# The same instructions on tiles that stand in another order in SBUF (a graph network in split fp32r products, one core)

## The reference

```python
h   = x @ W0 + b0                          # 256x256 weights
x1  = layernorm(x + (adj @ h) / adj.sum(-1, keepdims=True))
y1  = relu(adj @ (x1 @ W1) + b1)
y2  = relu(adj @ (y1 @ W2) + b2)
y3  = adj @ (y2 @ W3) + b3
out = layernorm(x1 + y3)                   # no gain, no bias, eps 1e-5
```

## Time and profile before

| | |
|---|---|
| median of three runs | 562.41 us |
| the profiled execution: its time | 563.61 us |
| its span in the trace | 561.8 us |
| TensorE busy with matmuls | 540.8 us, 3648 matmuls |
| TensorE busy with weight loads | 499.1 us, 3648 loads |
| VectorE, ScalarE, GpSimd busy | 356.8, 273.7, 197.8 us |

### The profile page before, as it was taken

One profiled execution on the slowest core, in us unless ns is written; L12 is line 12 of the kernel. 1 busy time (PEld: TensorE's weight loads), 2 busy tenths in 40 slices (PEclk: granted clock), 3 DMA queues, 4 the chain that ended last, 5 costly groups with the idle time before them and its releaser, 6 DMA issues.

```text
span 561.8 us, 10399 instructions
## 1 busy us (share of the span) xinstructions
PE 540.8 (96%) x3648; PEld 499.1 (89%) x3648; DVE 356.8 (64%) x1082; ACT 273.7 (49%) x645; POOL 197.8 (35%) x216
## 2 busy tenths in 40 slices
PE   3789999999999999999999999999999999999996
PEld 3768998989989898998989999898998989899885
DVE  4586575766747566674757657576674756657555
ACT  4156536454453645446364543645445364543532
POOL 1131807135090622608054180713509063261000
PEclk9899999999999999999999999999999999999999
DMA  6531050320505013050410405022050501300002
GB/s 204 189 90 62 1 187 2 101 88 1 188 0 179 8 55 132 0 187 0 134 52 24 163 0 187 0 90 97 0 187 0 175 13 54 134 1 39 1 1 75
DMA packets 19525, 43.53 MB, mean 77 GB/s; under 512 B 1968, under 2 KB 10928, under 8 KB 19504
## 3 DMA queue, kind: packets, MB, share of 16 engines
q1 hardware_dynamic: 19360, 43.00, 22.8%
q10 hardware_dynamic: 144, 0.26, 0.2%
HBM read 34.87 MB, written 8.39 MB: 77 GB/s over the span
## 4 chain that ended last, share of the span: by engine, by line
PE 92%; DVE 3%; DMA 2%; ACT 1%; issue 1%; SPq 0%; DVEq 0%
PE bank_b L154 16%; PE bank_a L154 15%; PE bank_b L155 15%; PE bank_a L156 15%; PE bank_a L155 15%; PE bank_b L156 15%; DMA adj_raw<-in_adjT 1%; DMA xT_raw<-in_xT 1%; DVE adj_lo L496 1%; DVE v L544 0%; DVE x_lo L496 0%; DVE stats L552 0%; DVE x L548 0%; DVE h_lo L496 0%; SPq L169 0%
## 5 line engine op out<-in xcount | busy, mean ns | idle before, releaser
L686 POOL TENSOR_TENSOR adj_lo<-adj_raw,adj_hi 128x512 fp32r<-128x512 f32 x56 | 70.9, 1299 | 281.6 <-ACT adj_hi L347 281.6
L496 DVE TENSOR_TENSOR x_lo<-bank_a,x_hi 128x512 fp32r<-128x512 f32 x64 | 44.3, 692 | 68.3 <-ACT bank_a L410 68.3
L154 PE MATMUL bank_b<-h_hi,adj_hi 128*128 128x258 f32 x256 | 73.3, 286 | 5.7 <-DVE h_lo L496 3.9
L155 PE MATMUL bank_b<-h_lo,adj_hi 128*128 128x258 f32 x256 | 73.4, 287 | 0.0
L156 PE MATMUL bank_b<-h_hi,adj_lo 128*128 128x258 f32 x256 | 72.7, 284 | 0.0
L154 PE MATMUL bank_b<-s_hi,adj_hi 128*128 128x256 f32 x256 | 71.8, 280 | 0.9 <-DVE s_lo L496 0.9
L155 PE MATMUL bank_b<-s_lo,adj_hi 128*128 128x256 f32 x256 | 71.4, 279 | 0.0
L156 PE MATMUL bank_b<-s_hi,adj_lo 128*128 128x256 f32 x256 | 71.4, 279 | 0.0
L385 ACT ACTIVATE std<-moments,eps_col 128x1 f32<-128x1 f32 x64 | 18.9, 295 | 101.2 <-DVE moments L560 101.2
L428 ACT ACTIVATE std<-moments,eps_col 128x1 f32<-128x1 f32 x64 | 18.9, 295 | 81.8 <-DVE moments L600 81.8
L679 POOL TENSOR_TENSOR x1b<-x,b_all 128x256 f32<-128x256 f32 x64 | 46.0, 752 | 30.6 <-DVE x L548 30.6
(11 more groups left out here) (72 smaller groups left out, 1551.4 us busy)
## 6 DMA issues: line engine op xcount, KB each, us to landing
adj_raw<-in_adjT SPq DMA_DIRECT2D x32, 512.0 KB, 5.5
xT_raw<-in_xT SPq DMA_DIRECT2D x32, 256.0 KB, 5.8
x_raw<-in_x SPq DMA_DIRECT2D x16, 512.0 KB, 6.4
out_y<-y SPq DMA_DIRECT2D x15, 512.0 KB, 2.9
w_raw<-in_w SPq DMA_DIRECT2D x3, 256.0 KB, 6.1
out_y<-y SPq DMA_DIRECT2D x4, 128.0 KB, 1.9
w_raw<-in_w ACTq DMA_DIRECT2D x1, 256.0 KB, 2.7
b_all<-in_b SPq DMA_DIRECT2D x2, 128.0 KB, 7.2
```

Source lines behind the costliest of these rows:

```text
L154: pe.matmul(acc, st[0], mv[0], start=start, stop=False)
L155: pe.matmul(acc, st[0], mv[1], start=False, stop=False)
L496: return dve.tensor_tensor(lo, full, hi.bitcast(F32), ALU.subtract)
L686: pool.tensor_tensor(adj_lo[:, s, k, :], adj_raw[:, k, :], adj_hi[:, s, k, :].bitcast(F32), ALU.subtract).then_inc(adj_split, 1)
```

## The change

The declarations of eight names are put in another place. No instruction, wait, shape, type or loop is changed.

```diff
         w_hi, w_lo = pair("w", [P, 4, KF, F])
+        xT_hi, xT_lo = pair("xT", [P, KF, N])
         adj_hi, adj_lo = pair("adj", [P, RING, T, N])
+        h_hi, h_lo = pair("h", [P, T, F + ONES])
         x1_hi, x1_lo = pair("x1", [P, T, F])
-        s2_hi, s2_lo = pair("s2", [P, T, F])
-
-
-        inv_rows = sb("inv_rows", [P, T], F32)
-        std1 = sb("std1", [P, T], F32)
-
-        xT_hi, xT_lo = pair("xT", [P, KF, N])
         g_hi, g_lo = pair("g", [P, KF, N])
         x2_hi, x2_lo = pair("x2", [P, KF, N])
+        s2_hi, s2_lo = pair("s2", [P, T, F])
         x3_hi, x3_lo = pair("x3", [P, KF, N])
         s3_hi, s3_lo = pair("s3", [P, T, F])
-        h_hi, h_lo = pair("h", [P, T, F + ONES])
...
         y = sb("y", [P, T, F], F32)
+        inv_rows = sb("inv_rows", [P, T], F32)
         stats1 = sb("stats1", [P, T, 6], F32)
...
         moments2 = sb("moments2", [P, T, 2], F32)
+        std1 = sb("std1", [P, T], F32)
         std2 = sb("std2", [P, T], F32)
```

## The result

The changed kernel takes 566.73 us, the median of four runs (566.22 to 567.36), against 562.4 us for the kernel before (562.33 to 563.61): a ratio of 1.0073, with a 95% interval of 1.0055 to 1.009. It is slower by 3 to 5 us, and the forecast was 566.9.

What follows compares the result with a forecast made beforehand. TensorE, never waiting mid-run, was taken as the bound, time being the sum of matmul pitches. Only p2 and p5 added, +4.5 us, to the median 562.41, giving 566.9 us; range 557.5 to 571.0, the forecast's own 564.5 to 568.5.

Steps and rivals of the forecast that it cites:

- p2 and p5: 512-column products, stationary x1 or s2, moving adj: 5.60 us each, +0.28 us a step, +4.5 us in all.
- "I take the pair", the rests modulo 128: All products: pitch judged by whether both operands' starts are odd or even multiples of 64 bytes; no size of its own.
- p3, p4, p6, p7 at 0: Products whose operands keep their rests: no change; bounds -0.40 us a step for p6, p3, p7, +0.11 for p4.
- p0 at 0: 256-column product whose operands come to the same rest: no change; at most 0.01 us a step gained, 0.10 lost.
- p1 at 0: 258-column product reading h and adj: no change; bounds -4.1 us and +0.6 us over 16 graphs.
- VectorE and the others at 0: VectorE, ScalarE and GpSimd on moved tiles: no change; 7% more VectorE work uncovered at the ends is about 1 us.
- Placement is inert: All products: level comes from product order alone, step stays 33.39 us, time 562.4 us; chance 0.25.
- Faster through `h`: p1 falls to 114.3 ns, -0.25 us a step, 558.3 us; includes p6, p3 or p7 dropping; chance 0.20.
- Slower still: p2 and p5 at 233.3 ns, p0 and p4 at 117.9 too: +3.4 us on top, 570.3 us; chance 0.10.
- rival 3: Same as Slower still: p0 and p4 at 117.9 ns add +3.4 us, 570.3 us; chance 0.10.
- rival 2: Same as Faster through `h`: p1 faster, 558.3 us; its side part is p6, p3 or p7 dropping; chance 0.20.
- theory A: From the experiments' expectations, all products: operand starts set the pace, and the product ahead passes its level on; no single size.

Runs made afterwards that it cites:

- x1_s2_64_clean: Kernel before with x1 and s2 moved by 64 bytes, every other large tile kept modulo 256: 565.31 us against 563.21, ratio 1.0032.
- same_rests: Tile order of the kernel after, unused spacers restoring the starts modulo 128 of the kernel before: 563.01 us against 563.05, ratio 0.9996.
- same_rests_256: Tile order of the kernel after, eight unused spacers restoring the starts modulo 256 of the kernel before: 563.11 us against 563.21, ratio 0.9997.
- the sweeps: Two separate programs, TensorE alone, groups of 12 matmuls: one varies the stationary start, the other also the moving start; 512 columns at multiples of 256 bytes: 226.6 to 226.7 ns.
- x1_s2_even: Kernel after with x1 and s2 put back on multiples of 128 by spacers: 565.92 us against 563.05 for the kernel before, ratio 1.005.
- sweep_rest: Separate program, TensorE alone, stationary start 0 to 1024 bytes past the moving one, steps of 32, up and back; 256 columns at 64 bytes: 118.1 or 113.8 ns.
- g0_s3_192: Kernel before with spacers putting g at 0 and s3 at 192 modulo 256: 565.68 us, ratio 1.0043.

## Why the prediction was right, and where it was wrong

- **The time: 566.9 forecast, 566.73 measured.** The closeness of the two is luck. The step grew by 0.20 us and not by 0.28, and what made up the 0.20 was not the sum that the forecast wrote down. The step explains 3.2 of the 4.3 us between the medians; the other 1.1 isn't in it, and is of the size of the spread between executions (562.33 to 563.61 for the kernel before).
- **p2 and p5: right, in place and size.** 5.60 us each was forecast, and 5.60 each is what they take, 233.3 ns a matmul. That a distance of 64 bytes costs this is borne out by the sweep (233.4 ns at 64, 227.8 to 226.7 at 0) and by x1_s2_64_clean. This term alone is the forecast's +4.5 us. The row that it took the price from fits only by luck: modulo 256, p3 stands at 192 and not at 64. At 192 the sweep has 229.2 to 230.2 ns, and p3 itself takes 229.0 in the kernel after and 233.6 in the kernel before, with the same two operands at the same distance. At 229.2 to 230.2 ns the same sum would have given +1.3 to +2.1 us, by estimate.
- **"I take the pair", the rests modulo 128: wrong.** The period is 256 bytes: same_rests missed p2 by 0.15 us, same_rests_256 missed nothing. The places of p2 and p5 are the same by either rule, since `x1` and `s2` went from distance 0 to 64; the likeness to p3 holds by the rule of 128 alone.
- **p3, p4, p6, p7 at 0: wrong, by -0.36 us a step for p3, p6 and p7 and +0.11 for p4.** The prediction saw the passing on in the rows near the end and gave bounds for it, -0.40 and +0.11, which both came about almost in full. It should have carried them into the likeliest case: it forecast a new pace for p2 and, behind it, old paces for products that it had seen take theirs in part from the product ahead. x1_s2_64_clean shows that.
- **p0 at 0: wrong by +0.14 us a step.** Its operands came to distance 0, where 256 columns take 119.1 to 120.0 ns in the sweeps and 119.8 here. The prediction took 0 because p0 was at the lower level already and its two rests became the same; the sweep shows that 256 columns are slow at 0, where 512 are fast. Its upper bound (117.9 ns) was too low as well. Own distance and passing on both lead there: p0 took 2.875 us at distance 0 behind a slow p7 (x1_s2_even), and 2.828 at its old distance in x1_s2_64_clean.
- **p1 at 0: nearly right**, +0.03 us. Its reason, that `h_lo` and the rows stay off the multiples of 64, no run tests by itself.
- **VectorE and the others at 0: right**, 471, 452 and 422 ns.
- **The rivals.** Placement is inert (0.25): out, and with it the rule of no change that the prediction drew from the Trainium skill. The Trainium skill's page "SBUF — State Buffer", section "Who interferes with whom", says that the two read ports are independent; in sweep_rest, with TensorE alone, the pitch of 512 columns depended on the distance between what the two read, 227.8 against 233.4 ns, and the measurement decides. Faster through `h` (0.20): p1 didn't gain, but the other half of that rival, p6, p3 and p7 down to the lower level, happened (-5.8 us in 16 graphs) and was outweighed. Slower still (0.10): its p0 and p4 at the slow pace happened too (+4.0 us). So what came was the forecast's term, somewhat more than rival 3 adds to it (3.4) and the side part of rival 2 at once, and these two came to -1.8 us together.

What stays open is the mechanism below the pitch. The runs show that the pace hangs on the distance modulo 256, on the number of columns and on something that the work ahead hands over. They don't show what is shared between the two reads, and no experiment was made that could. Nor is there a rule for the passing on: theory A's simple form (slow after fast, fast after slow) failed in g0_s3_192, where p7 at a distance of 64 stayed slow behind a p3 of 2.748 us, while it was fast behind one of 2.803. Nor does the length of the product ahead decide: at distance 64, p0 took 2.732 behind a p7 of 5.653 and 2.826 behind one of 5.656.

## What to carry to other kernels

When TensorE is busy all the time and two products of the same shape have different pitches, compare the starts of the stationary and the moving operand modulo 256 bytes before anything else, and do it in the product's own width. A declaration that is added, dropped or moved shifts every tile behind it, so an edit elsewhere can move the time through this alone, here by up to 1.2% between layouts; before a small gain is put down to an edit, give the tiles back their starts modulo 256 and measure again. To tune it, read the time of each product from the timeline, since the total hides terms that cancel, and try whole layouts: g0_s3_192 sped up one product and lost more behind it.

## What the runs showed of the hardware

- Back-to-back fp32r matmuls of 256 columns, each with its own weight load, took 113.3 to 120.5 ns at the full granted clock, and those of 512 columns 226.6 to 234.0 ns, depending on the distance between the two operands' starts and on what ran before. The dependence repeats every 256 bytes and is there with no other engine at work.
- At a distance of 64 bytes, 256 columns have two steady paces, 113.8 and 118.1 ns in the sweep, and which it is depends on what ran before; 512 columns have 233.4 only. At 192 bytes the products in the kernels have two as well: p7 5.653 and 5.440 us (117.8 and 113.3 ns), p3 2.803 and 2.748 us (233.6 and 229.0 ns). At 0 it is the wider one that is fast (226.7) and the narrower one that is slow (120.0).
- The products' lengths are reproducible to 1 ns from step to step and between two different layouts with the same starts modulo 256, in spite of all that the other engines and the DMA queues do beside them.
